# Attention scores from each head's own 32 rows, the far bias as extra rows of the same product, and one exponential over two PSUM banks

## The reference, cut to what matters

```python
qkv = x @ w_qkv.T
q, k, v = ...                                   # (B=4, H=16, N=512, D=8) each
scores = jnp.einsum('bhqd,bhkd->bhqk', q, k) * D ** (-0.5)
scores = scores + compute_bias(N, N, rel_bias_table)   # 32 buckets; constant beyond a distance of 91
attn = jax.nn.softmax(scores, axis=-1)
out = jnp.einsum('bhqk,bhkd->bhqd', attn, v)
out = out @ w_proj.T + b_proj
```

## Time and profile before

| what | value |
|---|---|
| median of 3 runs | 752.35 us (750.46 to 754.37) |
| span of the profiled execution | 825.8 us |
| TensorE matmul busy | 585.7 us, 71% |
| VectorE busy | 457.7 us, 55% |
| ScalarE busy | 352.9 us, 43% |
| GpSimd busy | 244.0 us, 30% |
| one step of the tree loop | 28.8 us |
| one step with the second layer's attention | 38.4 us |

### The profile page before, as it was taken

The page is one execution under the profiler, slowest core; times in us unless marked ns, Lnnn a source line. Parts: engine busy times, 40 slices in busy tenths (PEclk is TensorE's granted clock), DMA queues, the critical chain, the costliest instruction groups (busy, mean ns, idle before and its releaser), DMA issues.

```text
span 825.8 us, 13091 instructions
## 1 busy us (share of the span) xinstructions
PE 585.7 (71%) x3521; PEld 421.9 (51%) x3524; DVE 457.7 (55%) x1036; ACT 352.9 (43%) x1087; POOL 244.0 (30%) x201
## 2 busy tenths in 40 slices
PE   1376346199999534999999999999599988127700
PEld 0354233176667332676667667666366665127700
DVE  3879756057766401767766766675366567104500
ACT  4600011176657212676666658557165634012300
POOL 2006647500000668500006500008200000686065
PEclk9796586599999855999999999999799999559865
DMA  7997411133443413733345643312100000479433
GB/s 229 240 185 265 108 47 54 38 103 103 114 108 108 122 49 52 160 102 110 103 116 113 143 107 102 108 55 36 17 1 1 0 15 0 125 177 240 145 67 65
DMA packets 108827, 83.31 MB, mean 101 GB/s; under 512 B 8688, under 2 KB 105840, under 8 KB 108768
## 3 DMA queue, kind: packets, MB, share of 16 engines
q1 hardware_dynamic: 89952, 66.91, 29.8%
q0 software_dynamic: 15104, 12.63, 8.2%
q10 hardware_dynamic: 3712, 3.16, 1.3%
HBM read 58.30 MB, written 24.36 MB: 100 GB/s over the span
## 4 chain that ended last, share of the span: by engine, by line
PE 53%; issue 10%; another core or an unknown queue 5%; DVE 4%; ACT 4%; SPq 3%; POOL 3%; DMA 2%; DVEq 0%; POOLq 0%; ACTq 0%
PE ps L985 7%; PE ps L973 7%; PE ps L975 7%; PE ps L962 6%; PE ps L1040 4%; PE ps L948 3%; POOL acc L352 3%; PE ps L1050 3%; DVE ps L571 3%; PE ps L1111 2%; PE ps L1034 2%; PE ps L1092 2%; ACT pt L762 2%; SPq L210 2%
## 5 line engine op out<-in xcount | busy, mean ns | idle before, releaser
L571 DVE CUSTOM_DVE_ANT_0 ps<-ps,strip 128x512 f32<-128x512 f32 x256 | 176.7, 704 | 163.5 <-PE ps L962 125.6
L762 ACT ACTIVATE pt<-ps,far 128x164 f32<-128x164 f32 (+2 forms) x384 | 153.5, 412 | 67.5 <-PE ps L975 54.7
L347 POOL DMA_INDIRECT xs<-xr,slot x64 | 64.3, 1005 | 299.0 <-issue 138.1
L973 PE MATMUL ps<-qs,km 128*128 128x512 f32 x256 | 123.4, 482 | 29.3 <-ACT pt L762 20.9
L352 POOL DMA_INDIRECT yt<-ys,slot x48 | 74.0, 1541 | 196.2 <-DMA ys<-yl 182.2
L962 PE MATMUL ps<-km,qs 128*128 128x512 f32 x256 | 109.6, 444 | 9.7 <-DVE qs L553 3.9
L762 ACT ACTIVATE pt<-ps 128x220 f32<-128x220 f32 (+1 forms) x256 | 102.9, 402 | 22.2 <-remote 12.1
L975 PE MATMUL ps<-u_lo,rev_r 128*128 128x220 f32 (+1 forms) x256 | 75.4, 295 | 0.0
L973 PEld LDWEIGHTS ps<-qs,km 128*128 128x128 f32 x256 | 49.4, 193 | 48.9 <-ACT pt L762 27.5
L975 PE MATMUL ps<-u_hi,rev_r 128*128 128x220 f32 (+1 forms) x256 | 73.8, 288 | 0.0
L985 PE MATMUL ps<-pt,v_aug 128*32 128x512 f32 x512 | 69.1, 612 | 0.8 <-ACT pt L762 0.8
(11 more groups left out here) (191 smaller groups left out, 922.7 us busy)
## 6 DMA issues: line engine op xcount, KB each, us to landing
wt<-in_wl SPq DMA_DIRECT2D x144, 128.5 KB
xl<-xs SPq DMA_DIRECT2D x36, 258.0 KB
ys<-yl SPq DMA_DIRECT2D x36, 256.0 KB
xs<-mx SPq DMA_DIRECT2D x2, 3096.0 KB, 22.4
strip<-bias_bf SPq DMA_DIRECT2D x1, 3584.0 KB
yt<-xs SPq DMA_DIRECT2D x12, 258.0 KB, 3.4
strip<-in_wl SPq DMA_DIRECT2D x24, 128.5 KB
strip<-in_wl ACTq DMA_DIRECT2D x24, 128.5 KB
```

Source lines behind the costliest of these rows:

```text
L347: pool.indirect_dma_start(out=xs[t % 2][:, :], out_offset=bass.IndirectOffsetOnAxis(ap=slot[:, t, k:k + 1], axis=0), in_=xr[:, k, :], in_o ...
L571: V.tensor_tensor_reduce(out=bank(u % banks), in0=bank(u % banks), in1=strip[:, HG * g + j, b0:b0 + NS], scale=1.0, scalar=LOWEST, op0=ALU ...
L762: last = A.activation(pt[:, kt % 2, j, a:b_], ps[:, 2 + u % 2, a:b_], ACT.Exp, bias=c)
L973: T.matmul(bank(2 + u % 2), km[:, par, j, kt * P:(kt + 1) * P], qs[:, par, :], start=True, stop=False)
```

## The change

Four edits go together.

The keys are no longer masked. `km` (four copies) goes, `ks` becomes double, and both score products read only the 32 rows of their head: rows 32j to 32j+31 in `scores_k`, the first 25 of them in `scores_q`.

The bias left of the window against that right of it is carried by six of the head's rows (25 to 30). They are added to `qs` and `ks` by a second, bf16 matmul in each projection: `ql` and `kl` are the new weights, `qkr` the moving operand. The right-hand bias is subtracted from the whole table before the window's bias is made from it. A new routine on GpSimd, `far_rows`, builds these tiles in the preamble.

The exponential then needs no cuts. Every second unit, one ACTIVATE reads banks 2 and 3 together, 1024 columns, and counts for two units.

Some waits move with this: TensorE's first product waits for GpSimd's subtraction, ScalarE's first projection copy waits for the bias tables, which now lie in `qs` and `ks`, and the first projection waits for `far_rows`.

```diff
@@ constants and buffers
-        km = sb("km", [P, 2, HG, NS], F32R)
-        ks = sb("ks", [P, NS])
+        ks = sb("ks", [P, 2, NS], F32R)
@@ SyncE: far is loaded before the weights
@@ GpSimd, new (core)
+            def far_rows():
+                pool.wait_ge(S["d_far"], 32)
+                pool.wait_ge(S["d_f"], 48)
+                G.tensor_tensor(tab_s, tab_s, far[0:BUCKETS, 0, :], ALU.subtract).then_inc(S["tab_in"], 1)
+                settle(G.tensor_tensor(fc[:, 0], far[:, 1, :], far[:, 0, :], ALU.subtract))
...
+                settle(G.memset(ql[:], 0.0))
+                settle(G.memset(flat(kl[:]), 0.0))
+                settle(G.memset(flat(qkr[:]), 0.0))
...
+                G.affine_select(qkr[:, 0, :], qkr[:, 0, :], [[-1, NS]], ALU.is_ge, 0.0, base=P - SAT - 1, channel_multiplier=P
+                                ).then_inc(S["aug"], 1)
@@ before the addition of the projection's bias
+            far_rows()
@@ VectorE
             def split_k(n, par):
                 dve.wait_ge(S["h"], 2 * n + 1)
-                dve.wait_ge(S["km"], HG * n + 1)
-                V.scalar_tensor_tensor(ks[:], ks[:], col(C_LK), bank(PJ[1]), ALU.mult, ALU.add).then_inc(S["ks"], 1)
-                dve.wait_ge(S["ks"], n + 1 + CREDIT["ks"])
-                for j in range(HG):
-                    V.tensor_scalar(km[:, par, j], ks[:], col(C_HEAD + j), col(C_ONE + j), ALU.mult, ALU.add
-                                    ).then_inc(S["km"], 1)
+                V.scalar_tensor_tensor(ks[:, par], ks[:, par].bitcast(F32), lkc[:, 0:1], bank(PJ[1]), ALU.mult, ALU.add
+                                       ).then_inc(S["ks"], 1)
@@ ScalarE
             def exps(n, g, u):
                 kt, j = divmod(u, HG)
+                if u % 2 == 0:
+                    return
                 act.wait_ge(S["p2"], U * n + u + 1 + CREDIT["p2"])
                 act.wait_ge(S["pv"], KT * n + kt - 1 + CREDIT["pv"])
-                lo, hi = window(kt)
-                cuts = [(a, b_, c) for a, b_, c in ((0, lo, far[:, 1, HG * g + j:HG * g + j + 1]), (lo, hi, 0.0),
-                                                    (hi, NS, far[:, 0, HG * g + j:HG * g + j + 1])) if b_ > a]
-                for a, b_, c in cuts:
-                    last = A.activation(pt[:, kt % 2, j, a:b_], ps[:, 2 + u % 2, a:b_], ACT.Exp, bias=c)
-                last.then_inc(S["ex"], 1)
+                A.activation(pt[:, kt % 2, j - 1:j + 1, :], ps[:, 2:4, :], ACT.Exp).then_inc(S["ex"], 2)
@@ TensorE
-                T.matmul(bank(PJ[which]), (wq_s, wk_s)[which][:, g, :], xnT[:, bass.ds(b * NS, NS)], start=True, stop=True
+                T.matmul(bank(PJ[which]), (wq_s, wk_s)[which][:, g, :], xnT[:, bass.ds(b * NS, NS)], start=True, stop=False)
+                T.matmul(bank(PJ[which]), kl[:, g, :] if which else ql[:], qkr[:, which, :], start=False, stop=True
                          ).then_inc(S["proj"], 1)
...
-                T.matmul(bank(u % banks), qs[:, par, qt * P:(qt + 1) * P], backward(km[:, par, j, :]), start=True, stop=True
+                r = slice(HR * j, HR * j + MAXED)
+                T.matmul(bank(u % banks), qs[r, par, qt * P:(qt + 1) * P], backward(ks[r, par, :]), start=True, stop=True
                          ).then_inc(S["p1"], 1)
...
-                T.matmul(bank(2 + u % 2), km[:, par, j, kt * P:(kt + 1) * P], qs[:, par, :], start=True, stop=False)
+                r = slice(HR * j, HR * j + HR)
+                T.matmul(bank(2 + u % 2), ks[r, par, kt * P:(kt + 1) * P], qs[r, par, :], start=True, stop=False)
```

More of the change, by code:

```diff
@@ L33 @@
 H, D = 16, 8
+MAXED = 25
 HG = 4
@@ L144, in build @@
         cbt = sb("cbt", [P, 2, P], BF16)
+        rowm = sb("rowm", [P, HR])
+        lkc = sb("lkc", [P, 1])
+        fc = sb("fc", [P, 2, H])
+        fb = sb("fb", [P, 3, H], BF16)
+        ql = sb("ql", [P, P], BF16)
+        kl = sb("kl", [P, NG, P], BF16)
+        qkr = sb("qkr", [P, 2, NS], BF16)
         xr = sb("xr", [P, NT, ROW])
@@ L223, in _ @@
             sp.dma_start(tab_s, table).then_inc(S["d_f"], 16)
+            for i, bucket in enumerate((BUCKETS // 2 - 1, BUCKETS - 1)):
+                sp.dma_start(far[:, i, :], bass.AP(tensor=table.tensor, offset=bucket * H, ap=[[0, P], [1, H]])
+                             ).then_inc(S["d_far"], 16)
             sp.dma_start(bpb, bass.AP(tensor=bp.tensor, offset=0, ap=[[0, P], [1, P]])).then_inc(S["d_w"], 16)
@@ L340, in _, with settle @@
             pool.memset(v_aug[:].rearrange("p a b c d -> p (a b c d)"), 1.0).then_inc(S["ones"], 1)
+            done = [0]
+            def settle(ins):
+                done[0] += 1
+                ins.then_inc(S["pl"], 1)
+                pool.wait_ge(S["pl"], done[0])
+            G = nc.gpsimd
+            def far_rows():
[3 more added lines that the diff above has]
+                settle(G.tensor_tensor(fc[:, 0], far[:, 1, :], far[:, 0, :], ALU.subtract))
+                settle(G.tensor_copy(fb[:, 0], fc[:, 0]))
+                settle(G.tensor_tensor(fc[:, 1], fc[:, 0], fb[:, 0], ALU.subtract))
+                settle(G.tensor_copy(fb[:, 1], fc[:, 1]))
+                settle(G.tensor_tensor(fc[:, 0], fc[:, 1], fb[:, 1], ALU.subtract))
+                settle(G.tensor_copy(fb[:, 2], fc[:, 0]))
+                settle(G.memset(fc[:, 0], 0.0))
+                for k in range(3):
+                    last = G.tensor_copy(fc[HR * k:HR * k + HR, 0], fb[HR * k:HR * k + HR, k])
+                    settle(last)
+                pool.wait_ge(S["d_c"], 32)
+                ident_jr = cst[:, C_ID:C_ID + P].rearrange("p (j r) -> p j r", r=HR)
+                settle(G.tensor_tensor(rowm[:], ident_jr[:, 0], ident_jr[:, 1], ALU.add))
+                settle(G.tensor_tensor(rowm[:], rowm[:], ident_jr[:, 2], ALU.add))
+                settle(G.tensor_tensor(rowm[:], rowm[:], ident_jr[:, 3], ALU.add))
+                settle(G.tensor_tensor(lkc[:], cst[:, C_LK:C_LK + 1], rowm[:, 28:29], ALU.subtract))
+                settle(G.tensor_tensor(lkc[:], lkc[:], rowm[:, 29:30], ALU.subtract))
+                G.tensor_tensor(lkc[:], lkc[:], rowm[:, 30:31], ALU.subtract).then_inc(S["lkc"], 1)
+                settle(G.memset(ql[:], 0.0))
+                settle(G.memset(flat(kl[:]), 0.0))
+                settle(G.memset(flat(qkr[:]), 0.0))
+                three = lambda a, n: a.unsqueeze(1).unsqueeze(1).to_broadcast([P, n, 2, 3])
+                cells = lambda a: a.rearrange("p (h r) -> p h r", r=HR)[:, :, 25:31].rearrange("p h (two k) -> p h two k", two=2)
+                settle(G.tensor_copy(cells(ql[:]), three(cst[:, C_ID:C_ID + 3], HG)))
+                settle(G.tensor_tensor(cells(flat(kl[:])), fc[:, 0].unsqueeze(2).unsqueeze(2).to_broadcast([P, H, 2, 3]),
+                                       three(rowm[:, 0:3], H), ALU.mult))
+                settle(G.tensor_copy(tok(qkr[:, 1])[:, 1:KT], rowm[:, 0:3].unsqueeze(2).to_broadcast([P, 3, P])))
+                ones_at = flat(kl[96:97]).rearrange("p (h r) -> p h r", r=HR)[:, :, 24:25]
+                settle(G.memset(ones_at, 1.0))
+                settle(G.memset(qkr[96:97, 1, :], 1.0))
+                settle(G.memset(qkr[:, 0, :], 1.0))
+                G.affine_select(qkr[:, 0, :], qkr[:, 0, :], [[-1, NS]], ALU.is_ge, 0.0, base=P - SAT - 1, channel_multiplier=P
+                                ).then_inc(S["aug"], 1)
@@ L662, in _ @@
             dve.wait_ge(S["d_u"], 48)
+            dve.wait_ge(S["lkc"], 1)
             split_k(0, 0)
@@ L740, in high @@
                 act.wait_ge(S["proj"], 2 * n + 2 - which)
[L741 to L746, removed]
+                act.wait_ge(S["p2"], U * n + 1)
+                A.activation((qs, ks)[which][:, par], bank(PJ[which]), ACT.Copy).then_inc(S["h"], 1)
             def values(n, b, g, par):
@@ L832, in _ @@
             act.wait_ge(S["ones"], 2)
+            act.wait_ge(S["d_b"], 48)
             high(0, 1, 0)
```

24 lines of the change are left out of this document (10 added, 14 removed), and 2 rows, old and new, of the table S.

## The result

The changed kernel takes 1218.9 us, the median of 4 runs (1208.7 to 1228.46), against 753.36 us for the kernel before beside it (4 runs, 750.46 to 755.23). The ratio is 1.6126, with a 95% interval of 1.6037 to 1.6214. The forecast of 904 us and its range of 835 to 935 were wrong by some 300 us, in the direction forecast.

A forecast was written before the change was run, and what follows sets the result against it. TensorE was taken to bound the steps. A tree step would gain 8.2 + 4.1 + 0.2 = 12.5 us, 151.5 us over all steps, added to the 752.35 us median: 904 us, range 835 to 935.

The forecast's parts named there:

- The clock falls: Rival: TensorE's new idle time halves its clock in 12 steps, up to 28 us each, over 1,200 us in all; chance 0.04.
- Changes of mode: Score products over 32 rows between 128-row products: 18 ins-and-outs of 0.23 us, 4.1 us a step.
- The exponential over two banks: Behind odd units TensorE waits 1.06 us of a 1.43 us chain; 8.2 us a tree step, ACTIVATE 1.08 us.
- VectorE's copies: Four masked copies of 0.54 us a step go from VectorE; gain taken at nothing, at most 24 us.
- second projection product: Two more bf16 products of 512 columns a step; the keys' one hidden, the queries' one costs 0.23 us.
- ScalarE's relief: ScalarE busy 100 us less or more, none of it on the path; faster exponentials could win 0.4 us a step.
- Steps 0 and 4: Tree steps where stretches with nearly all but GpSimd standing hide part of the waits; counted by half, 12.5 us together.
- GpSimd's preamble: Some 26 small instructions before the first scatter, hidden in 44.9 us of idle time; cost nothing.
- Steps 13 and 14: Other work covers the exponential, so no wait is added, only changes of tiling mode, 8 us; steps near 42 us.
- Side by side: Rival: score products in different bands run in fours, saving 5.5 us a step, 88 us, to 664 us; chance 0.04.

The follow-up runs named there:

- e1: The changed kernel with both score products over all 128 rows (heads mix, exponent scaled by 1/1024), two-bank exponential kept; 867.39 us, ratio 1.1521 to the kernel before.
- e2: The changed kernel with one exponential of 512 columns for each unit again, score products still over 32 and 25 rows; 881.49 and 907.62 us.
- e3: The changed kernel with score products over all 128 rows (heads mix, exponent scaled) and one exponential for each unit; 752.05 us, ratio 0.9993 to the kernel before.
- e10: The changed kernel with nine stages each one slot later, behind odd units, bands and two-bank exponential kept; 976.01 us, ratio 1.2997 to the kernel before.
- e6: The changed kernel with score products over all 128 rows (heads mix, exponent scaled), two-bank exponential, stages moved behind odd units; 796.26 us, ratio 1.0548 to the kernel before.
- e8: The changed kernel with two extra 512-column products over the head's own 32 rows before each odd unit's `scores_q`; 1258.74 us, ratio 1.6761 to the kernel before.

## Why the prediction was wrong

**The failed step: the clock.** The prediction gave "The clock falls" a chance of 0.04 and took 1.0 in the steps, from windows in which the kernel before was 72% busy and from the fact that it had fallen only behind a long idle stretch. These rows all have products over 128 rows. They could not say what the clock does beside products over 32, and this was exactly what changed. In its place: 0.55 to 0.67 in the tree steps, some 200 us that neither part has alone. The price of that rival, over 1,200 us, was right by luck: it had 336 us for the clock (12 steps of 28 us on top of 904, 1,240 us) where the runs have some 200, and what it had for the rest, 151.5 us, is 245 and more in e1 and e2.

**Changes of mode: the mechanism right, mis-sized, and enough by itself to miss.** Forecast 4.1 us a step, measured 7.7 with single exponentials (e2 against e3) and 5.7 with the two-bank ones (e10 against e6). The in-and-out of `weigh` costs 0.23 us. For `scores_q` it is about 0.29 (0.09 in, 0.20 out), for `scores_k` with the late `u_lo` behind it about 0.39 (0.09, 0.18 and 0.12); in e2, where no two-bank wait covers any, more of the 32 lie open than the 18 I counted. The losses of e1 and e2 added to e3 are 997 us at the least, so the range to 935 would have been missed at full clock too. The Trainium skill, TensorEngine Tiling (Array Packing), Key Properties, has TensorE drain at a change of mode: the rows agree for bands of rows as well, with 0.42 us from `scores_k` to `u_hi` where it was 0.24.

**The exponential over two banks: right.** 1.47 us for the chain against 1.43, an ACTIVATE of 1025 ns against 1080, 8.8 us a tree step (e1 against e3) against 8.2. That VectorE's copies, ScalarE's shorter work and the second projection product together are worth nothing that can be measured is e3: ratio 0.9993. I overrated ScalarE's relief: 58.6 us less busy, not 100. Steps 0 and 4 I counted by half, from stretches of the trace before which the traces of e1 and e3 do not have: these two steps took 54.6 and 71.3 us there and 31.0 and 32.5 in e3, and e1 takes 8.3 and 7.5 us more than e3 in them, nearly the 8.8 of the other steps. At the forecast's own price the term was 25 us and not 12.5.

**GpSimd's preamble: hidden,** as forecast. Timeline of the kernel after, its first scatter: the 40.88 us of idle time stand where 44.88 stood. It starts 2.4 us later than before, and e3, which has the same preamble, is no slower.

```profile
68.55 1.20 POOL L404 DMA_INDIRECT xs<-xr,slot  x1 [40.88 <-DVE xr L594]
```

**Steps 13 and 14:** forecast near 42 us. Step 14 is 48.7 at full clock. e2 has 9.0 us of its 10.3 (47.18 against 38.21), e1 1.2: the waits were rightly taken to be nearly nothing there, the changes of mode were at twice my price.

**Side by side:** it exists (e2), worth some 1.7 us a step together with the changes of mode that it saves, and not the 5.5 of the rival, since it needs a `scores_q` and a `scores_k` next to each other.

**What stays open.** What exactly makes the clock fall and return isn't settled: in the changed kernel it comes back at 780 us in a stretch that looks like others in which it does not (790 to 804, without idle time too). In e2 it fell without any idle time of TensorE, and there one execution had much of this and the other little. The runs show that rows and waits both count, and not by which measure.

## What to carry to other kernels

A product over 32 rows that stands between products over 128 is not cheaper than one over 128 rows with zeros in the masked ones: it streams as long (in e8 three in a row and the way out take 0.90 us, 0.23 each with 0.20 for the way out), pays 0.3 to 0.4 us for going in and out, and puts TensorE's clock at risk. In the main part, kernels with full rows had it fall only behind several us in which TensorE stood nearly idle; kernels with bands had it fall behind waits of about 1 us, and e2 behind none. An instruction that reads two PSUM banks at once gives up their double buffering; it needs other TensorE work, as long as itself, right behind the second bank. And edits of which one leaves the clock alone (the waits) and the other lowers it only now and then (the bands) can hold it down together, so price the clock for the sum of the edits, not for each.

## What the runs showed of the hardware

The granted clock stayed at 1.00 with full-row products and TensorE at 79% (29.84 of 37.76 us), and stood at 0.64 with 32-row products, the same waits and TensorE at 92% (56.24 of 61.40; the share is high partly because the slow clock makes every product longer). With 32-row products and no idle time at all it fell to 0.50 and stayed there for some 48 us (e2, from about 262). Two extra products of 128 rows at each of 8 places raised the mean from 0.68 to 0.72 and 0.76; the same with 32 rows left it at 0.67 to 0.68. A product behind one that has just left a band starts later by 0.12 us, even though it is the second of full size in a row.
